# Query features and linear attention in tiled fp32 products in place of split products, with the order of the FFN phase written as words

## The chip, the cores and the metric

The kernel runs on one core of a Trainium2 chip. The metric is the device time of one execution in microseconds (us). The engines are named as the profile does: PE (TensorE, matrix products), DVE (VectorE), ACT (ScalarE), POOL (GpSimd), SP (SyncE, which issues all DMA transfers).

## The reference

Eight sequences ("pairs" below, since each is two tiles of 128 rows) of 256 tokens, width 512, 16 heads of 32. All in fp32:

```
xn = layernorm(x);  q = xn Wq' + bq;  k = ctx Wk' + bk;  v = ctx Wv' + bv      (16 heads of 32)
q' = relu(q_h Wqf');  k' = relu(k_h Wkf') * mask                                (64 features a head)
kv = k'^T v;  k_sum = sum k'                                                    (64 x 32, 64 a head)
x  = x + (q' kv / (q' k_sum + 1e-8)) Wo' + bo
x  = x + BitNet FFN of layernorm(x): 8 bit activations, ternary weights,
     up * relu(gate)^2, sub-layernorm, quantized again, down (512 -> 2048 -> 512)
```

## The kernel before

A planner (`Plan`, L79) takes every instruction as a step with its lane, its waits and a cost. PE's steps run in the order in which the code adds them. ACT, DVE, POOL and SP are ordered by list scheduling: a time by which PE needs each step is worked out backwards from PE's order with the table `COST`, and each engine takes what is ready and needed first. Semaphores are derived from the plan.

Products that need fp32 accuracy are written as three float32r products of high and low parts (`products`), so each operand has to be split on ACT (high) and DVE (low). A phase for the keys comes first (until about 125 us): for each pair, keys, values, key features (`features`, L546, already fp32 products in tiles of 32 rows by 64 columns, one for each of four row groups and two column groups) and the blocks k'^T v with k_sum in a 33rd column (`kv`, L566, tiles of 128 rows by 64 columns), kept in `kvc` for all pairs.

Then come eight pairs on the query side, with these blocks for pair a, named by their letters in the code after the change:

- X (`s1`, twice): transposes of the normalized rows, 4 each. W (`s2`): q, 48 products of 256 columns, then on ACT the bias and high part (`qoh`), on DVE the low part (`qol`), and from pair 2 on a further copy `qy` and four SBUF to SBUF DMA copies `qx`, `qy` that put high and low parts of two heads side by side.
- Q (`s3`): query features, 24 products of 256 columns in pairs 0 and 1, 16 from pair 2 on. ACT writes relu as the high part, DVE the low part (`aph`, `apl`, at a = 0 `wkh`, `wkl`).
- K (`kv_blocks`): high and low parts of this pair's kv, two heads side by side with zeros between (`kvh`, `kvl`).
- A (`s4`, once for each row tile): attention, for each of 8 head pairs 3 products of 66 columns, so 48 in all; DVE adds 1e-8, takes reciprocals and multiplies (`dn`, `rd`, `on`).
- T (`s5`): 4 transposes of the attention rows, high and low parts. S (`s6`): output projection, 12 products of 512 columns, then on DVE, POOL and ACT the residual, layernorm and quantization, and the DMA transpose `xqT`, on which the FFN of that row tile waits.
- L (`ln1`): layernorm of the next pair's rows into `xn`, the tile that A's rows also use.
- G i.h (`gate_up`): half h of the gate and up products of row tile i, 8 + 8 bf16 products of 512 columns. D i (`down`): 16 such products. The FFN runs one pair behind the attention.

`mix(main, side, lag, end)` spreads the side list over the main list. In the loop at L924 the 48 attention products of a pair, with the transposes T of its first row tile among them, are spread over G and D products, from 6 after the first on to 10 before the last. For pair 0 they are spread over values products. Pair 7 is ordered by the string `TAIL`. PSUM banks 0 to 3 belong to G, banks 4 to 7 are handed out in turn by `bank()`. Lines of the profile: L344 is the helper of nearly all products, L347 that of ACT, L350, L353 and L356 those of DVE, L612 the transposes, L581 `kv` and L558 `features`.

Of the kernel before, what the change touches and what calls it, by code (L numbers as in the profile page):

```python
# [10 lines left out]
F32 = mybir.dt.float32  # L11
# [25 lines left out]
TAIL = "D9 G12.0:a Q0123 K MG12.0:b,G12.1,D10 S0 S1 G13.0 G13.1 G14.0 G14.1 G15.0 G15.1 B012345 D11 D12 D13 D14 D15"  # L37
# [34 lines left out]
HOLDS = ("Y", "xbo", "kvh", "kvl")  # L72
HELD = ("kk", "kvl", "xn", "xm", "yb", "yk")
# [156 lines left out]
def xattn_bitffn_kernel(nc, x_d, ctx_d, wk_d, wv_d, wq_d, wo_d, feat_d, small_d, bv_d, bo_d, g_d, wg_d, wu_d, wd_d, out_d):  # L230
# [4 lines left out]
    with ExitStack() as es:  # L235
# [193 lines left out]
        dma("feat", 0.25, [], fraw, feat_d, "feat")  # L429
# [58 lines left out]

        def biased(tag, oqs, outs, k, bias, copy=None):

            for oq, src in zip(oqs, outs):
                act(f"{tag}.{oq}.hi", 0.4, [k, "small"], qoh[:, T * oq:T * oq + T], src, ACT.Identity, bias=bias[:, oq:oq + 1])
                if copy is not None:
                    act(f"{tag}.{oq}.copy", 0.4, [k, "small"], copy[:, T * oq:T * oq + T], src, ACT.Identity, bias=bias[:, oq:oq + 1])
            los = []
            copies = [f"{tag}.{oq}.copy" for oq in oqs] if copy is not None else []
            for oq, src in zip(oqs, outs):
                qs = slice(T * oq, T * oq + T)
                los.append(stt(f"{tag}.{oq}.lo", 0.4, [f"{tag}.{oqs[-1]}.hi", f"{tag}.{oq}.hi", k, "small"] + copies, qol[:, qs], src, bias[:, oq:oq + 1], f32(qoh[:, qs]), ALU.add, ALU.subtract))
            return los  # L500
# [45 lines left out]
        def features(b):  # L546


            for t in range(2):
                i = 2 * b + t  # L550
                for q in range(4):
                    for r in range(4):
                        for c in range(2):
                            waits = [f"kT{b}.{q}.all", "feat.raw"] + (bank_user[r] if t == q == c == 0 else [])
# [4 lines left out]
            for r in range(4):  # L559
# [3 lines left out]
                ready = [f"kf{2 * b + 1}.3.{r}.0", f"kf{2 * b + 1}.3.{r}.1", "small", "feat.raw", "feat.hi", "fpad.lo"]  # L563
                bank_user[r] = [stt(f"kf{b}.{r}.rows", 0.65, ready, dst, src, 0.0, on, ALU.max, ALU.mult)]

        def kv(b):  # L566
# [3 lines left out]
            for half in range(2):  # L570
                for pr in range(4 * half, 4 * half + 4):
                    for t in range(2):
                        for hd in range(2):
                            def call(half=half, pr=pr, t=t, hd=hd):
                                i = 2 * b + t
                                waits = [f"kf{b}.{r}.rows" for r in range(4)] + [f"v{b}.{t}.rows"] + (bank_user[base + half] if pr % 4 == t == hd == 0 else [])
                                rows = slice(64 * hd, 64 * hd + 64)
                                out = ps[rows, base + half, 33 * (pr % 4):33 * (pr % 4) + 33]
                                o = 256 * (2 * (pr % 2) + hd) + 64 * (pr // 2)
                                left, right = kp[:, t, o:o + 64], vt[:, i % 4, pr, 33 * hd:33 * hd + 33]  # L580
                                k = add("pe", f"kv{b}.{pr}.{t}.{hd}", 0.06, waits, lambda e: e.matmul(out, left, right, start=t == 0, stop=t == 1, tile_position=(0, 64 * hd)))  # L581
                                if pr % 4 == 3 and t == hd == 1:
                                    src = ps[:, base + half, 0:132].rearrange("p (c d) -> p c d", c=4)
                                    bank_user[base + half] = [act(f"kv{b}.{half}", 0.3, [f"kv{b}.{pr}.{t}.0", k], kvc[:, b, 4 * half:4 * half + 4, :], src, ACT.Copy)]
# [441 lines left out]
```

How the kernel before makes its waits and increments, by code:

```python
        def run(lane, eng):  # L199
            seen = {}
            for i in order.get(lane, []):
                _, name, _, waits, fn, dma = self.steps[i]
                need = {}
                for w in waits:
                    s, v = at[w]
                    if need.get(s, (0, None))[0] < v:
                        need[s] = (v, w)
                for s, (v, _) in need.items():
                    if seen.get(s, 0) < v:
                        eng.wait_ge(s, v)
                        seen[s] = v
                last = fn(eng)
                if dma is not None:
                    last.then_inc(dma_sems[dma], 16)
                elif name in at:
                    last.then_inc(sems[lane], 1)
# [6 lines left out]
        def sync(e):  # L223
            run("sp", e)
            e.wait_ge(dma_sems["out"], issued["out"])
```

## Time and profile before

| | |
|---|---|
| median of 3 runs | 454.1 us (453.23 to 454.24) |
| profiled execution | 454.95 us, span 453.2 us |
| PE busy | 439.6 us (97%), 4147 records |
| weight loads (PEld) | 342.4 us (76%) |
| DVE busy | 367.0 us (81%) |
| ACT busy | 298.0 us (66%) |
| POOL busy | 130.7 us (29%) |
| DMA | 45.61 MB, mean 101 GB/s |
| granted TensorE clock | 1.00 throughout |

The span runs from the first to the last instruction. Products are pipelined, so a record's busy time is longer than the distance between two starts; the distance is the cost. The last 44 us have no attention left.

### The profile page before, as it was taken

Reading aid. Unit: us, or ns where it says so; the run is one execution under the profiler, and the core shown is the slowest. Engines: PE = TensorE matmul, PEld = TensorE weight load, DVE = VectorE, ACT = ScalarE, POOL = GpSimd, SP = SyncE. Lnnn points to the kernel's source line nnn. Section 1 sums busy time; section 2 is a strip of 40 time slices with the busy share of each in tenths; the row PEclk is TensorE's granted clock in tenths of the full one; section 3 lists DMA queues with packets and bytes.
Section 4 is the critical chain, followed back from the end, with each engine's and each line's share of the span. In section 5 each row is a group of like instructions: output and inputs, shape, how many; then the busy total and the mean of one; then the engine's idle time right before and its main releaser. Section 6 shows DMA issues by size and latency. Waiting matters only on the chain.

```text
span 453.2 us, 10053 instructions
## 1 busy us (share of the span) xinstructions
PE 439.6 (97%) x4147; PEld 342.4 (76%) x4147; DVE 367.0 (81%) x635; ACT 298.0 (66%) x426; POOL 130.7 (29%) x280
## 2 busy tenths in 40 slices
PE   8999899999999999999999999999999999899995
PEld 5888889888999878958767776796877777684443
DVE  4735929358966989999989999898999898898992
ACT  5766969764232276786686768578575975738982
POOL 0000000005420644342342541444235054224430
PEclk9999999999999999999999999999999999999999
DMA  7991917423400210251223225025122123233045
GB/s 237 417 381 48 346 77 244 175 88 106 184 3 24 94 25 0 48 128 37 48 71 69 54 44 115 23 48 128 37 46 57 39 46 58 72 82 58 14 106 149
DMA packets 53085, 45.61 MB, mean 101 GB/s; under 512 B 43440, under 2 KB 44336, under 8 KB 51120
## 3 DMA queue, kind: packets, MB, share of 16 engines
q1 hardware_dynamic: 53040, 44.98, 34.1%
q8 instruction: 32, 0.52, 0.5%
q14 instruction: 13, 0.11, 0.1%
HBM read 27.14 MB, written 4.19 MB: 69 GB/s over the span
## 4 chain that ended last, share of the span: by engine, by line
PE 71%; DVE 13%; ACT 8%; issue 3%; DMA 2%; POOL 1%; SPq 0%; DVEq 0%; ACTq 0%
PE ps L344 63%; ACT rb L347 4%; PE ps L581 3%; DVE zb L350 3%; PE ps L558 3%; DVE tk L788 2%; PE ps L612 2%; ACT rbe L347 2%; ACT zb L347 1%; DMA xs<-in_wk_dram 1%; DVE qol L350 1%; DVE yqb L815 1%; ACT aph L347 1%; DMA yqTq<-yqb 1%; DMA xqT<-xqb 1%
## 5 line engine op out<-in xcount | busy, mean ns | idle before, releaser
L344 PE MATMUL ps<-tg,xqT 128*128 128x512 bf16 x256 | 68.1, 386 | 1.0 <-DMA xqT<-xqb 1.0
L344 PE MATMUL ps<-tu,xqT 128*128 128x512 bf16 x256 | 68.2, 385 | 0.0
L344 PE MATMUL ps<-td,yqT 128*128 128x512 bf16 x208 | 50.7, 385 | 0.0
L347 ACT ACTIVATE rb<-zb 128x1024 f32<-128x1024 f32 x29 | 30.6, 1055 | 28.8 <-DVE zb L350 28.8
L353 POOL TENSOR_SCALAR tk<-tk 128x1 f32<-128x1 f32 x96 | 37.4, 390 | 41.2 <-DVE tk L739 21.3
L347 ACT ACTIVATE zb<-zb,cm,tk 128x1024 f32<-128x1024 f32 x29 | 34.8, 1235 | 14.8 <-POOL tk L350 14.8
L347 ACT ACTIVATE rb<-ps 128x1024 f32<-128x1024 f32 x29 | 29.6, 1020 | 19.0 <-PE ps L344 18.1
L344 PEld LDWEIGHTS ps<-tu,xqT 128*128 128x128 bf16 x256 | 25.1, 98 | 21.5
L344 PE MATMUL ps<-kvh,apl 128*128 128x66 f32 x112 | 41.1, 367 | 0.0
L344 PE MATMUL ps<-kvh,aph 128*128 128x66 f32 x112 | 40.3, 359 | 0.3 <-DVE apl L356 0.3
L344 PE MATMUL ps<-kvl,aph 128*128 128x66 f32 x112 | 40.4, 361 | 0.0
L344 PEld LDWEIGHTS ps<-tg,xqT 128*128 128x128 bf16 x256 | 24.1, 99 | 21.0 <-issue 1.9
L350 DVE TENSOR_TENSOR zb<-zb,g_b 128x1024 f32<-128x1024 f32 x30 | 37.0, 1232 | 2.9 <-ACT rb L347 2.4
L350 DVE TENSOR_TENSOR zb<-ps,rb 128x1024 f32<-128x1024 f32 x29 | 35.2, 1213 | 4.5 <-PE ps L344 3.4
L350 POOL TENSOR_TENSOR tk<-tk 128x1 f32<-128x1 f32 x32 | 15.4, 480 | 78.7 <-ACT rb L347 65.3
L344 PE MATMUL ps<-aph,wkh 128*128 128x256 f32 x128 | 36.1, 286 | 0.9 <-ACT wkh L347 0.9
L788 DVE TENSOR_REDUCE tk<-zb 128x1 f32<-128x1024 f32 x30 | 36.4, 1212 | 0.3
L344 PE MATMUL ps<-aph,wqh 128*128 128x256 f32 x128 | 36.0, 282 | 0.3 <-DVE apl L350 0.3
L344 PE MATMUL ps<-apl,wkh 128*128 128x256 f32 x128 | 35.2, 279 | 0.7 <-issue 0.7
L350 POOL TENSOR_TENSOR xs<-xs,bo_b 128x512 f32<-128x512 f32 x16 | 24.5, 1540 | 39.0 <-DMA bo_b<-in_bo_dram 19.6
L344 PE MATMUL ps<-aph,wql 128*128 128x256 f32 x128 | 35.7, 279 | 0.0
L344 PE MATMUL ps<-apl,wqh 128*128 128x256 f32 x128 | 35.7, 279 | 0.0
(149 smaller groups left out, 1262.3 us busy)
## 6 DMA issues: line engine op xcount, KB each, us to landing
xs<-in_wg_dram SPq DMA_DIRECT2D x4, 1024.0 KB, 13.3
xs<-in_wu_dram SPq DMA_DIRECT2D x4, 1024.0 KB, 6.7
xs<-in_wd_dram SPq DMA_DIRECT2D x4, 1024.0 KB, 8.0
xs<-in_x_dram SPq DMA_DIRECT2D x8, 512.0 KB, 5.6
out_dram<-xs SPq DMA_DIRECT2D x15, 256.0 KB, 2.2
craw<-in_ctx_dram SPq DMA_DIRECT2D x7, 512.0 KB, 7.2
qoh<-qol SPq DMA_DIRECT2D x12, 128.0 KB, 2.2
qy<-qol SPq DMA_DIRECT2D x12, 128.0 KB, 2.4
```

The costliest lines, as they stand in the source:

```text
L344: return add("pe", name, cost, waits, lambda e: e.matmul(out, lhsT, rhs, start=start, stop=stop))
L347: return add("act", name, cost, waits, lambda e: e.activation(out, in_, func, **kw))
L350: return add(lane, name, cost, waits, lambda e: e.tensor_tensor(out, a, b, op))
L353: return add(lane, name, cost, waits, lambda e: e.tensor_scalar(out, a, s1, s2, op0, op1))
L558: add("pe", f"kf{i}.{q}.{r}.{c}", 0.015, waits, lambda e, out=out, left=left, right=right, at=(32 * r, 64 * c): e.matmul(out, left, right, ...
L581: k = add("pe", f"kv{b}.{pr}.{t}.{hd}", 0.06, waits, lambda e: e.matmul(out, left, right, start=t == 0, stop=t == 1, tile_position=(0, 64 ...
L612: add("pe", f"{tag}.{kc}", 0.11, (waits + bank_user[b] + ["small"]) if kc == 0 else [], lambda e, out=out, src=src: e.transpose(out, src, ...
L788: add("dve", f"ym{u}", 1.15, [f"Y{u}"], lambda e: e.tensor_reduce(col(M0 + h, i), zs, AX_X, ALU.max, apply_absolute_value=True))
L815: add("dve", f"yb{v}", 0.6, [f"yk{v}"] + war, lambda e, dst=dst, z=z: e.tensor_scalar(dst, z, MAGIC, None, ALU.subtract))
```

## The change

Query features and attention become plain fp32 products in tiles, as the key features were, and the split operands go with them.

- W writes q once, on ACT, with the bias, as fp32 `qT` (at a = 0 into `kT`). The low parts, the copy `qy` and the DMA copies are gone.
- Q is 16 products in 32x64 tiles with 256 moving columns: for each half of the quads, four row groups (heads) by two column groups. It needs four banks. ACT writes relu once, four steps of 512 columns, into `qf`.
- A is 64 products for a pair in 64x64 tiles with 33 moving columns straight from `kvc`: 8 head pairs, 2 heads (row groups), 2 column groups of 64 tokens, for each row tile. Each head parity has a bank of its own. K is gone with its memsets.
- `kvc` holds heads h and h + 4 together (`head`), so that rows 0 to 63 and 64 to 127 fit `qf`.
- A writes its rows to a tile of its own, `rows_of` (at a = 0 still `xn`), so L waits for the transposes X of the pair before.
- The order of pairs 1 to 7 is the list `FLOW`. Attention is no longer spread over FFN products: it stands in one piece between two halves.
- The feature weights are loaded directly into `fkr`, without the casts.

```diff
-TAIL = "D9 G12.0:a Q0123 K MG12.0:b,G12.1,D10 S0 S1 G13.0 G13.1 G14.0 G14.1 G15.0 G15.1 B012345 D11 D12 D13 D14 D15"
+FLOW = (
+    "G0.0:a Q G0.0:b A0 A1 G0.1 T0 T1 G1.0 G1.1 L S0 X0 X1 S1 W0 W1 D0",
+    "G2.0:a Q G2.0:b A0 A1 G2.1 T0 T1 D1 G3.0 G3.1 L S0 X0 X1 S1 W0 W1 D2",
...
+    "G10.0:a Q G10.0:b A0 A1 G10.1 T0 T1 G11.0 G11.1 L S0 X0 X1 S1 W0 W1",
+    "D9 G12.0:a Q G12.0:b A0 A1 G12.1 T0 T1 D10 S0 S1 G13.0 G13.1 G14.0 G14.1 G15.0 G15.1 B012345 D11 D12 D13 D14 D15",
+)
...
-HOLDS = ("Y", "xbo", "kvh", "kvl")
-HELD = ("kk", "kvl", "xn", "xm", "yb", "yk")
+HOLDS = ("Y", "xbo")
+HELD = ("kk", "xn", "xm", "yb", "yk")
...
-        dma("feat", 0.25, [], fraw, feat_d, "feat")
+        dma("feat", 0.2, [], fkr[:, :], feat_d[:, 0:384], "feat")
...
-                war = [f"oT{i - 2}.3"] if a else [f"warm{WARM - 1}"]
+                war = [f"oT{i - 2}.3" if a == 1 else f"xT{i - 2}.3"] if a else [f"warm{WARM - 1}"]
...
-                bank_user[b] = biased(f"qT{a}", (2 * o2, 2 * o2 + 1), [ps[:, b, 0:256], ps[:, b, 256:512]], k, bq, qy if a > 1 else None)
-                if a > 1:
-                    qs = slice(512 * o2, 512 * o2 + 512)
-                    dma(f"qx{a}.{o2}", 0.125, bank_user[b], f32(qoh[64:128, qs]), f32(qol[0:64, qs]), f"qx{o2}")
-                    dma(f"qy{a}.{o2}", 0.125, bank_user[b], f32(qy[0:64, qs]), f32(qol[64:128, qs]), f"qy{o2}")
+                bank_user[b] = [act(f"qT{a}.{oq}.all", 0.4, [k, "small"], (qT if a else kT)[:, T * oq:T * oq + T], ps[:, b, 256 * (oq % 2):256 * (oq % 2) + 256], ACT.Identity, bias=bq[:, oq:oq + 1]) for oq in (2 * o2, 2 * o2 + 1)]
+        def s3(a):
+            banks = [bank() for r in range(4)]
+            for q2 in range(2):
+                for r in range(4):
+                    for c in range(2):
+                        q = 2 * q2 + c
+                        rows, weights = slice(32 * r, 32 * r + 32), 256 + 64 * (r % 2)
+                        out = ps[64 * c:64 * c + 64, banks[r], 256 * q2:256 * q2 + 256]
+                        left, right = fkr[rows, weights:weights + 64], (qT if a else kT)[rows, T * q:T * q + T]
+                        waits = [f"qT{a}.{q}.all", "feat"] + (bank_user[banks[r]] if q2 == c == 0 else [])
+                        add("pe", f"qf{a}.{q2}.{r}.{c}", 0.0535, waits, lambda e, out=out, left=left, right=right, at=(32 * r, 64 * c): e.matmul(out, left, right, start=True, stop=True, tile_position=at))
+            war = [f"at{2 * a - 1}.7.1.{c}" for c in range(2)] if a else ctx_lo[NB - 1]
+            for r in range(4):
+                dst = qf[:, :].rearrange("p (q r t) -> p r q t", q=2, r=4)[:, r]
+                src = ps[:, banks[r], :].rearrange("p (q t) -> p q t", q=2)
+                bank_user[banks[r]] = [act(f"qf{a}.{r}.rows", 0.5, [f"qf{a}.1.{r}.0", f"qf{a}.1.{r}.1"] + war, dst, src, ACT.Relu)]
+        def s4(a, t):
+            i = 2 * a + t
+            banks = [bank(), bank()]
+            for pr in range(NP):
+                for hd in range(2):
+                    for c in range(2):
+                        rows, o = slice(64 * hd, 64 * hd + 64), T * pr + P * t + 64 * c
+                        waits = [f"qf{a}.{pr}.rows"] if pr < 4 and hd == c == 0 else []
+                        if pr == c == 0:
+                            waits = waits + bank_user[banks[hd]] + [f"kv{a}.0", f"kv{a}.1"]
+                        out = ps[64 * c:64 * c + 64, banks[hd], 33 * pr:33 * pr + 33]
+                        left, right = qf[rows, o:o + 64], kvc[rows, a, pr, :]
+                        add("pe", f"at{i}.{pr}.{hd}.{c}", 0.027, waits, lambda e, out=out, left=left, right=right, at=(64 * hd, 64 * c): e.matmul(out, left, right, start=True, stop=True, tile_position=at))
...
         features(last)
         listed += [6, 7]
         s2(0)
-        mix(main[4:8], [])
+        mix(main[4:12], [])
         listed += [0, 1, 2, 3]
         s3(0)
+        mix(main[12:18], [])
         listed += [0, 1, 2, 3]
-        mix(main[8:], s4(0, 0, 0.1) + s4(0, 1, 0.1), 4)
-        left = kv(last)
-        mix(left[:16], [])
+        s4(0, 0)
+        s4(0, 1)
+        mix(main[18:], [])
...
-        mix(left[16:], [])
+        mix(kv(last), [])
...
-            mix(main, side, 6, 10)
-            s5(a, 1)
...
+        for a, words in enumerate(FLOW, 1):
+            for word in words.split():
+                c, r = word[0], word[1:]
+                if c == "Q":
+                    s3(a)
+                elif c == "A":
+                    s4(a, int(r))
...
+                elif c == "W":
+                    s2(a + 1, (int(r),))
```

## Rows read from the trace of the kernel before

**Rows 1.** Windows: us, busy us (instructions) of each engine, granted clock, DMA

```profile
180.00:220.00 40.00, 40.00 (x262) 30.02 (x260) 37.73 (x67) 28.49 (x42) 15.52 (x32) 1.00 0.27 60
```

**Rows 2.** The page's chain that ended last, by engine

```profile
PE 71%; DVE 13%; ACT 8%; issue 3%; DMA 2%; POOL 1%; SPq 0%; DVEq 0%; ACTq 0%
```

**Rows 3.** Timeline of PE, pair 2: start, busy us, line, operation, count [idle before]

```profile
193.03 3.63 PE L344 MATMUL ps<-td,yqT 128*128 128x512 bf16 x16
...
199.76 0.47 PE L344 MATMUL ps<-qoh,fth 128*128 128x256 f32 x1
...
201.83 1.68 PE L344 MATMUL ps<-tg,xqT 128*128 128x512 bf16 x7
203.33 0.30 PE L344 MATMUL ps<-kvh,aph 128*128 128x66 f32 x1
...
212.75 0.60 PE L612 MATMUL ps<-small,xn 128*128 128x128 f32 x4
...
216.32 0.61 PE L344 MATMUL ps<-tg,xqT 128*128 128x512 bf16 x2
```

**Rows 4.** Timeline of PE, fp32 products in tiles, keys' side

```profile
107.13 2.06 PE L581 MATMUL ps<-vt,kp 128*64 128x33 f32 x64
109.12 0.50 PE L344 MATMUL ps<-woh,aph 128*128 128x512 f32 x1
...
112.07 1.60 PE L558 MATMUL ps<-fkr,kT 32*64 32x64 f32 x128
```

**Rows 5.** Timeline of PE, pair 0

```profile
132.12 0.28 PE L344 MATMUL ps<-qoh,fpd 128*128 128x256 f32 x1
...
134.95 0.40 PE L344 MATMUL ps<-woh,apl 128*128 128x512 f32 x1
...
136.11 0.19 PE L344 MATMUL ps<-kvh,wkh 128*128 128x66 f32 x1
...
144.03 0.31 PE L581 MATMUL ps<-vt,kp 128*64 128x33 f32 x4
...
148.16 0.50 PE L344 MATMUL ps<-woh,qoh 128*128 128x512 f32 x1 [0.55 <-DVE qol L350]
```

**Rows 6.** Timeline of PE, pair 1

```profile
167.92 0.38 PE L344 MATMUL ps<-kvh,aph 128*128 128x66 f32 x1
...
178.59 0.61 PE L344 MATMUL ps<-tg,xqT 128*128 128x512 bf16 x2
```

**Rows 7.** Timeline of PE, pair 7

```profile
386.04 1.89 PE L344 MATMUL ps<-tg,xqT 128*128 128x512 bf16 x8 [0.98 <-DMA xqT<-xqb]
388.49 0.35 PE L344 MATMUL ps<-qoh,fth 128*128 128x256 f32 x1 [0.57 <-issue]
...
391.79 0.38 PE L344 MATMUL ps<-kvh,aph 128*128 128x66 f32 x1
...
401.19 2.34 PE L344 MATMUL ps<-td,yqT 128*128 128x512 bf16 x10
```

**Rows 8.** Timeline of ACT

```profile
151.66 1.09 ACT L347 ACTIVATE aph<-ps 128x512 fp32r<-128x512 f32 x2 [3.48 <-PE ps L612]
...
163.64 1.02 ACT L347 ACTIVATE rb<-ps 128x1024 f32<-128x1024 f32 x1 [0.22 <-PE ps L344]
```

**Rows 9.** Timeline of DVE, the low parts of Wo

```profile
145.15 2.35 DVE L350 TENSOR_TENSOR wol<-xs,woh 128x1024 fp32r<-128x1024 f32 x2
```

**Rows 10.** Timeline of SP's queue

```profile
159.06 6.25 SPq L746 DMA_TRANSPOSE xqT<-xqb  x2
```

**Rows 11.** Groups by line, DVE: busy us, mean ns | idle before

```profile
L356 DVE SCALAR_TENSOR_TENSOR apl<-ps,aph 128x512 fp32r<-128x512 f32 x28 | 18.0, 683 | 0.9 <-ACT aph L347 0.9
```

**Rows 12.** Timeline of ACT, start of the last stretch

```profile
409.74 2.37 ACT L347 ACTIVATE zb<-zb,cm,tk 128x1024 f32<-128x1024 f32 x2 [5.13 <-POOL tk L350]
```

**Rows 13.** Timeline of PE, the last products

```profile
430.01 7.07 PE L344 MATMUL ps<-td,yqT 128*128 128x512 bf16 x32
...
446.72 3.67 PE L344 MATMUL ps<-td,yqTq 128*128 128x256 bf16 x32 [1.74 <-DMA yqTq<-yqb]
```

More of the change, by code:

```diff
@@ L487, in xattn_bitffn_kernel @@
         CW = wst[:, 12:13]
[L489 to L500, printed above, removed]
         def keys(b):
@@ L553, in features @@
                         for c in range(2):
-                            waits = [f"kT{b}.{q}.all", "feat.raw"] + (bank_user[r] if t == q == c == 0 else [])
+                            waits = [f"kT{b}.{q}.all", "feat"] + (bank_user[r] if t == q == c == 0 else [])
                             o = T * q + P * t + 64 * c
@@ L572, in kv, with call @@
                     for t in range(2):
-                        for hd in range(2):
-                            def call(half=half, pr=pr, t=t, hd=hd):
+                        for c in range(2):
+                            def call(half=half, pr=pr, t=t, c=c):
                                 i = 2 * b + t
[L576 to L582, printed above, removed]
+                                waits = [f"kf{b}.{r}.rows" for r in range(4)] + [f"v{b}.{t}.rows"] + (bank_user[base + half] if pr % 4 == t == c == 0 else [])
+                                h = head(pr, c)
+                                o = 256 * (h % 4) + 64 * (h // 4)
+                                out = ps[64 * c:64 * c + 64, base + half, 33 * (pr % 4):33 * (pr % 4) + 33]
+                                left, right = kp[:, t, o:o + 64], vt[:, i % 4, h // 2, 34 * (h % 2):34 * (h % 2) + 33]
+                                k = add("pe", f"kv{b}.{pr}.{t}.{c}", 0.06, waits, lambda e: e.matmul(out, left, right, start=t == 0, stop=t == 1, tile_position=(0, 64 * c)))
+                                if pr % 4 == 3 and t == 1 and c == 1:
                                     src = ps[:, base + half, 0:132].rearrange("p (c d) -> p c d", c=4)
-                                    bank_user[base + half] = [act(f"kv{b}.{half}", 0.3, [f"kv{b}.{pr}.{t}.0", k], kvc[:, b, 4 * half:4 * half + 4, :], src, ACT.Copy)]
+                                    bank_user[base + half] = [act(f"kv{b}.{half}", 0.3, [f"kv{b}.{pr}.1.{z}" for z in range(2)], kvc[:, b, 4 * half:4 * half + 4, :], src, ACT.Copy)]
                             calls.append(call)
@@ L616, in s1 @@
             i = 2 * a + t
-            b, k = transposes(f"xT{i}", t, [f"xn{i}"])
+            b, k = transposes(f"xT{i}", xn[:, t, :], [f"xn{i}"])
             src = ps[:, b, :].rearrange("p (a c) -> p a c", a=KC)
@@ L921, in xattn_bitffn_kernel @@
         s2(1)
-        kv_blocks(1)
-        for p in range(NB - 2):
-            a, n = p + 1, p + 2
-            early = (0, 1) if p == 0 else ()
-            s3(a, early)
-            mix(gate_up(2 * p, 0), [])
-            s3(a, [q for q in range(4) if q not in early])
-            if p:
-                kv_blocks(a)
-            side = s4(a, 0) + s4(a, 1)
-            side.insert(36, lambda: s5(a, 0))
-            main = gate_up(2 * p, 1) + (down(2 * p - 1) if 0 < p < NB - 3 else []) + gate_up(2 * p + 1, 0) + gate_up(2 * p + 1, 1)
-            mix(main, side, 6, 10)
-            s5(a, 1)
-            ln1(n)
-            s6(a, 0)
-            s1(n, 0)
-            s1(n, 1)
-            s6(a, 1)
-            s2(n)
-            if n < NB - 1:
-                mix(down(2 * p), [])
-        a = NB - 1
         rest = {}
```

164 lines of the change are left out of this document (49 added, 115 removed), and 3 rows, old and new, of the table FLOW.

## The prediction

> **What bounds the kernel now.** I read the windows first: between 180 and 220 us TensorE is busy for all 40.00 us and VectorE for 37.73, at granted clock 1.00 [rows 1]. The page's chain puts 71% of the span on PE and 13% on DVE [rows 2]. So until about 409 us the order of products on PE is the clock of the kernel: a product taken away is time gained, unless a wait takes its place. I then went through PE's timeline pair by pair [rows 3, 5 to 7], and last to the end, where ACT and DVE alternate on the chain.
>
> **The change, part by part, on PE.** *Old attention.* In pair 2, 48 attention products lie between the first at 203.33 and the last FFN products at 216.32, 12.99 us [rows 3]. The code puts 47 bf16 products there (64 in the mix, less 7 ahead and 10 behind). One costs 0.216 us (16 took 3.63, the last of them 0.38 by itself: 3.25/15) [rows 3], so 10.15; four transposes cost 0.43 (busy 0.60, less the 0.17 by which 3.63 exceeds 16 x 0.216). That leaves 2.4 us, 0.050 a product: spread out one by one they are cheap. Pairs 3 to 5 have the same mix. In pair 1 there are only 31 bf16 products to spread them over: 178.59 - 167.92 = 10.67, less 6.70 and 0.43, leaves 3.5 [rows 6]; pair 6 has the same mix. In pair 7, 401.19 - 391.79 = 9.40, less 23 x 0.216 and 0.46, leaves 4.0 [rows 7]. In pair 0 the stretch from 136.11 to 144.03 holds 11 values products of 0.232 ((136.11 - 134.95)/5) and leaves 5.4 [rows 5]. Sum: 5.4 + 2 x 3.5 + 4 x 2.4 + 4.0 = 26.0 us.
>
> *Old query features.* 24 products took 134.95 - 132.12 = 2.83 in pair 0 [rows 5]; pair 1 has the same 24. In pair 2, 16 took 201.83 - 199.76 = 2.07 [rows 3], and six pairs are like it: 12.4. Sum 18.1. Old total 44.1 us.
>
> *New products.* No query-side tile is in this trace, but the keys' side has fp32 products in tiles. Each appears as two records (64 in a features batch of the code, x128 in the row). In 32x64 tiles with 64 moving columns, 128 records take 1.60 us, 12.5 ns each; in 128x64 tiles with 33 columns, 64 take 2.06, 32 ns each [rows 4]. Block A of the new code has 64 products, 128 records, a pair, with 33 columns and four tiles in place of two. Bounds: 128 x 12.5 ns = 1.6 us (all four as parallel as the eight are) and 128 x 32 ns = 4.1 us (no better than the 128x64 ones). I take half of the second, 2.0, since twice as many tiles can be under way and the columns are the same. Block Q has 16 products, 32 records, of 256 columns. A 256-column fp32 record should stream 0.21 us, an estimate from the four transposes above (128 columns, 0.43/4 each, one record). With eight tiles side by side that is 32 x 0.21/8 = 0.85; with only the four row groups side by side 1.7. The 32x64 row speaks for more than four: 64 columns would stream 53 ns, and a record came every 12.5, so 4.3 in flight even with loads of weights on both sides of so short a product. I take 1.0. Going into or out of tiles costs 0.1: the product after the tiles is busy 0.50, where another of its kind takes 0.40 [rows 4, 5]. Four such edges a pair: 0.4. New sum per pair 2.0 + 1.0 + 0.4 = 3.4, times 8 is 27.2. Gross gain 44.1 - 27.2 = 16.9 us.
>
> The kernel's row of 12.5 ns a record also answers a floor on starts. The Trainium skill (TensorE: Matmul & The Clock Gate, "Wait — 56ns, not 53.3ns?") says that matmul starts never come closer than about 25 ns, however few columns. By that rule block A would take 128 x 25 ns = 3.2 us, 1.2 more a pair and 9.6 in all, and the time would be 452; this trace has records twice as dense as that, so it disagrees for tiles.
>
> **What takes part of it back.** *The wait in front of block A.* The new order is gate half of G, Q, up half of G (8 products, 1.73 us), A. A needs four Relu results on ACT, which come one after another: two 512-column ones took 1.09, 0.55 each [rows 8]. ACT first has the gate's own Relu, 1.02 [rows 8], which becomes ready just as Q starts and fills Q's 1.0. Then 4 x 0.55 + 0.3 of signalling = 2.5 us behind Q's end, against 1.73 + 0.1 + 0.4 (A's first twelve products) = 2.2: 0.3 of wait if ACT is free, and 1.3 if one more 1 us operation is ahead. ACT is busy 28.49 of 40 us [rows 1]. I take 0.7 a pair, bounds 0 and 2.0; 8 pairs, 5.6. Queued behind A's first product on PE is everything, so each of these waits is paid in full. *Pair 0.* S0 waits for the low parts of Wo, which can start only when the last values product is done; the two took 2.35 on DVE, and S0 started at 148.16 after 0.55 idle [rows 5, 9]. This distance stays, while the attention products that filled some of it go: 0.6 lost (0 to 1.5). *Pair 1.* The first FFN product now follows W directly. Before, it had 1.42 us of query features ahead of it, and the first xqT transpose was issued only at 159.06 [rows 10], on a chain that began with S0's end. S0's end to W's end stays the same, so up to 1.4 becomes visible; 0.7 taken, as DVE has less to do. Together 6.9.
>
> *What gets easier.* DVE loses the low parts of q, of the features (28 x 0.683 = 18.0 us in that row alone [rows 11]) and of the kv blocks. With 37.73 of 40 busy, DVE's queue is what makes things late. In pair 7 PE waited 0.98 for xqT and 0.57 in front of the query features, the place of the qx and qy copies that are gone [rows 7]: 1.5 gained (0 to 1.6). In the end stretch ACT starts late (idle 5.13, then two yk until 412.1) [rows 12] and has to be through the last gates; the last products start at 446.72 where PE alone, from 430.01 with four down blocks of 3.46, would be there at 443.9 [rows 13]. So at most 2.9 can come back, at least 0 since the order of words after pair 7's S1 is the same; I take 0.5. DMA copies qx, qy (SP), the two memsets (POOL) and three start-up casts (ACT) are hidden in the first two cases by the PE stretch beside them; removing them counts 0. ln1 writes to a tile of its own now and no longer waits for the output transposes; it had been on no wait of PE, 0. New planner costs only reorder ACT, DVE, POOL and SP; ACT's order is in the 0.7.
>
> Sum: 16.9 - 6.9 + 1.5 + 0.5 = 12.0. The profiled execution took 454.95, span 453.2, which is 0.85 over the median 454.1 of the runs shown. 454.95 - 12.0 = 442.95; by the median, 442.1. I say 442.
>
> **Rivals.** *A, tiles don't run side by side (ends slower).* The place is block A: if its records come every 32 ns as in the 128x64 row, it takes 4.1 instead of 2.0, 16.8 over all pairs, and 459; with Q at 1.7 as well, 464. It decides from 3.4 + 12.0/8 = 4.9 us a pair for Q, A and edges. For it: the old products, spread among bf16, cost only 0.050. Against it: the 12.5 ns row. *B, the waits take most of it.* Without the mix, each link Q, ACT, A, DVE, output transposes T stands in the open. At 2.0 in front of A and 0.3 at T it is 1.6 x 8 = 12.8 worse: 455, about the time before; at half of that, 448. For it: ACT runs operations of 1 us that can't be interrupted. Against it: ACT and DVE lose work. *C, no wait at all.* Q's results are in time, Wo and xqT too: 6.9 back, and the end gives 2.9: 433. *D, column tiles of one row group take turns.* The code issues both column tiles of a row group in succession, and Q takes 1.7: 5.6 worse, 448. The Trainium skill (TensorE: Matmul & The Clock Gate, "Part 3: Packing small matmuls — row/col tiling") says that a load of weights overlaps a running product only when its row group differs, which would make such turns. The 12.5 ns row has 4.3 records in flight at 53 ns, just over the four of that rule, so the trace doesn't exclude it.
>
> **How the numbers follow.** Forecast (waits near 0.7, tiles side by side) 0.53, its own range 437 to 446. A 0.10, B 0.12, C 0.12, D 0.13. The range that leaves out no more than 2 in 10 runs from 434 (close to C) to 453 (most of B). Within 0.2% (0.9 us, about what can be told from no change) lies a strip of B: 0.04. Slower: A and the rest of B, 0.11. Faster: 0.85.
>
> **What would show it.** In the timeline of PE, block A of pairs 2 to 5 should be 128 records within 2.0 us (4.1 is rival A), block Q 32 records within 1.0 (1.7 is D). Idle time of PE in front of A, released by ACT, of 0.3 to 1.3 (none is C, 2 is B). S1's end of pair 2 to that of pair 3 should shrink by 0.4 us only; the gain is at pairs 0, 1, 6 and 7. DVE's busy time between 180 and 220 should fall from 37.7 to near 33. The wait for xqT in pair 7 should be gone. The prediction is wrong if block A costs over 3 us, or if PE loses over 2 us in each pair to waits.

## The result, and the profile after

The kernel after takes 450.1 us (median of 4 runs, 449.26 to 450.7), the kernel before 454.17 (4 runs, 453.23 to 454.42). The ratio is 0.991, interval 0.9892 to 0.9928: faster by 0.9%, 4.1 us, where 12.0 was forecast. The profiled execution took 450.66 with a span of 448.6; before it was 454.95 and 453.2. So the span fell by 4.6.

First the windows (busy us of PE, PEld, DVE, ACT, POOL, then granted clock, DMA share, GB/s), which answer to [rows 1]:

```profile
180.00:220.00 40.00, 39.15 (x350) 25.31 (x354) 33.75 (x57) 25.17 (x35) 13.33 (x32) 1.00 0.31 61
...
380.00:420.00 40.00, 36.84 (x305) 19.80 (x308) 29.90 (x51) 26.48 (x34) 10.20 (x30) 0.96 0.22 50
```

DVE fell to 33.75, as forecast. But PE, which was busy for all 40.00 us, now stands still for 0.85 of them, and in the later window for 3.16, at a granted clock of 0.96. The page's chain shows the same, beside [rows 2]:

```profile
PE 44%; DVE 21%; ACT 14%; POOL 9%; issue 9%; DMA 3%; SPq 0%; DVEq 0%; ACTq 0%
```

PE's share fell from 71% to 44%. The work was removed from PE, and the chain now runs more often over DVE, ACT and POOL. Next PE's timeline in pair 0, where neither new block waits:

```profile
132.11 1.12 PE L643 MATMUL ps<-kT,fkr 32*64 32x256 f32 x32
133.16 0.50 PE L350 MATMUL ps<-woh,aph 128*128 128x512 f32 x1
...
134.75 2.35 PE L663 MATMUL ps<-kvc,qf 64*64 64x33 f32 x128
137.03 0.50 PE L350 MATMUL ps<-woh,aph 128*128 128x512 f32 x1
```

From start to start, block Q's 32 records take 1.05 us (1.0 forecast) and block A's 128 take 2.28 (2.0). With four edges of 0.1, Q and A cost 3.7 us in pair 0. Later on they are cheaper: in pair 2 (rows below) the stretch from G2.0's first product at 191.22 to the transposes T at 202.35 is 11.13 us. Less 32 FFN products of 0.216 and less the 0.97 that Q waits, 3.25 are left for Q, A and edges, against 3.4 forecast; A with its edges is 2.1 of it, 16 to 17 ns a record. The prices were nearly right; the loss lies between the blocks.

To place it, I cut the span at fixed points of PE's order: the first keys' product, the first S0 product of pair 0 (148.16 and 142.88), the eight transposes X (L605, before L612) of pairs 1 to 6, G13.0 (409.28 and 400.98), the end. X of pair 1 and of pair 6, before:

```profile
183.96 1.03 PE L612 MATMUL ps<-small,xn 128*128 128x128 f32 x8
...
371.92 1.04 PE L612 MATMUL ps<-small,xn 128*128 128x128 f32 x8
```

After:

```profile
178.49 1.03 PE L605 MATMUL ps<-small,xn 128*128 128x128 f32 x8
...
366.84 1.03 PE L605 MATMUL ps<-small,xn 128*128 128x128 f32 x8
```

| stretch (us) | before | after | change | forecast |
|---|---|---|---|---|
| to the first keys' product | 107.13 | 106.35 | -0.8 | 0 |
| to S0 of pair 0 | 41.03 | 36.53 | -4.5 | -3.5 |
| pair 1 (to its X) | 35.80 | 35.61 | -0.2 | -1.5 |
| pairs 2 to 5 (X to X) | 151.82 | 152.59 | +0.8 | -1.5 |
| pair 6 | 36.14 | 35.76 | -0.4 | -1.5 |
| pair 7 (to G13.0) | 37.36 | 34.14 | -3.2 | -3.5 |
| from G13.0 on | 43.92 | 47.62 | +3.7 | -0.5 |

The X of pair 5 stands at 335.78 and 331.08. The first line is no effect of the change: the start-up moves by up to 2.5 us between kernels that differ only later (S0 of pair 0 stands at 141.72 in experiment 2 and at 144.19 in experiment 6). Three places hold the miss: the end stretch (4.2), pairs 2 to 5 (2.3), pairs 1 and 6 (2.4).

**Pairs 2 to 5.** Pair 2 on all engines:

```profile
190.01 1.63 DVE L359 TENSOR_SCALAR xq<-xs,mv,rstd 128x512 f32<-128x512 f32 x1 [0.72 <-POOL rstd L356]
190.09 2.69 POOL L356 TENSOR_TENSOR xs<-xs,bo_b 128x512 f32<-128x512 f32 x2
...
191.22 1.89 PE L350 MATMUL ps<-tg,xqT 128*128 128x512 bf16 x8
...
191.56 1.76 DVE L774 TENSOR_SCALAR yqb<-zb 128x1024 bf16<-128x1024 f32 x1
...
193.04 0.67 PE L643 MATMUL ps<-qT,fkr 32*64 32x256 f32 x12
...
193.25 0.74 DVE L362 SCALAR_TENSOR_TENSOR xs<-ps,tk,xs 128x512 f32<-128x512 f32 x1
...
194.04 1.08 PE L643 MATMUL ps<-qT,fkr 32*64 32x256 f32 x20 [0.33 <-DVE xs L362]
...
202.35 1.04 PE L605 MATMUL ps<-small,rows_of 128*128 128x128 f32 x8
...
210.13 1.89 PE L350 MATMUL ps<-tg,xqT 128*128 128x512 bf16 x8
212.10 1.90 PE L350 MATMUL ps<-tu,xqT 128*128 128x512 bf16 x8
```

Q is broken after 12 of its records. Q needs four banks of PSUM; the fourth is the one in which the down block D stands, and it is free only when DVE has read D's result (the copy `y`, L362, to 193.99). From 193.04 to the end of Q at 195.12 are 2.08 us instead of 1.12: 0.97 lost (1.13 in pair 5). DVE comes late to `y` since two operations ahead of it take 1.63 and 1.76 us, while POOL adds `bo` to x (xbo, 2.69). The Trainium skill (SBUF — State Buffer, "SBUF: two separate sides") says that VectorE, when it works in a mode with two ports or reads two operands from SBUF, and GpSimd exclude each other from one shared pair of ports, and that the first holds it for its whole instruction. The rows look like that (1.63 and 1.76 us beside POOL's 2.69), and the third experiment below moves POOL's work away.

A second loss is smaller and no row gives it as idle time: the gate half of the second row tile starts at 210.13 and its up half at 212.10, 1.97 us for 8 products that take 1.73. That is 0.24 in each of pairs 2 to 5.

**Pairs 1 and 6.** In pair 1 PE waits in front of G0.0, within A and in front of an up half; in pair 6 block A is cut three times:

```profile
156.17 1.67 PE L350 MATMUL ps<-tg,xqT 128*128 128x512 bf16 x7 [0.97 <-DMA xqT<-xqb]
...
161.99 1.72 PE L663 MATMUL ps<-kvc,qf 64*64 64x33 f32 x104 [0.17 <-ACT qf L353]
...
173.99 1.90 PE L350 MATMUL ps<-tu,xqT 128*128 128x512 bf16 x7 [0.67 <-DVE sy L365]
```

```profile
348.90 0.31 PE L663 MATMUL ps<-kvc,qf 64*64 64x33 f32 x4 [0.31 <-ACT qf L353]
...
350.36 1.72 PE L663 MATMUL ps<-kvc,qf 64*64 64x33 f32 x104 [0.17 <-ACT qf L353]
...
362.35 1.90 PE L350 MATMUL ps<-tu,xqT 128*128 128x512 bf16 x7 [0.66 <-DVE zb L356]
```

A's wait in front and within makes its stretch 3.1, 3.6 and 3.5 us long in pairs 1, 6 and 7, so 1.0, 1.5 and 1.4 more than 2.1. The waits of 0.67 and 0.66 in front of G1.1's and G11.1's up halves (0.82 each from start to start) are new too, and were not in the forecast. The up half needs the banks that DVE empties of the half before; no experiment took this wait away, so why DVE is late there stays open.

**End stretch.** PE, then SP's queue:

```profile
410.12 3.30 PE L350 MATMUL ps<-tg,xqT 128*128 128x512 bf16 x8 [2.07 <-DMA xqT<-xqb]
...
415.26 1.89 PE L350 MATMUL ps<-tg,xqT 128*128 128x512 bf16 x7
```

```profile
405.08 1.83 SPq L781 DMA_TRANSPOSE yqT<-yqb  x1
406.96 6.84 SPq L705 DMA_TRANSPOSE xqT<-xqb  x2
```

G14.0 waits 2.07 us for the transpose xqT14, which stands behind yqT12 in SP's queue. Before, the order was the other:

```profile
413.35 1.20 SPq L746 DMA_TRANSPOSE xqT<-xqb  x1
414.65 1.72 SPq L822 DMA_TRANSPOSE yqT<-yqb  x1
```

Behind the wait the granted clock falls to half (the 1.2 GHz level):

```profile
411.00:412.00 1.00, 1.00 (x4) 0.36 (x3) 0.97 (x1) 0.70 (x1) 0.74 (x3) 0.50 0.00 0
...
413.00:414.00 1.00, 1.00 (x4) 0.34 (x3) 0.97 (x2) 0.54 (x1) 0.00 (x0) 0.58 0.17 35
```

G14.0's 16 products take 415.26 - 410.12 = 5.14 us; 16 products of G13.0 and G13.1 take 3.5 (402.71 to 406.17 is 3.46). So 2.07 of wait and 1.7 of clock make the 3.7 of the table. The two are not one cause, though. In experiment 3 the same wait stands, and the clock behind it stays at 1.00:

```profile
409.43 1.89 PE L350 MATMUL ps<-tg,xqT 128*128 128x512 bf16 x8 [2.07 <-DMA xqT<-xqb]
...
410.00:411.00 1.00, 1.00 (x7) 0.45 (x5) 0.97 (x2) 1.00 (x3) 0.45 (x2) 1.00 0.00 0
```

Experiments 2 (wait 2.07) and 6 (2.02) show no fall there either. The wait comes with the queue's order; the fall stood behind it in this execution and stands elsewhere in others.

### The profile page after: what moved, and what is told of

It is laid out like the page before. It is cut to its first block, busy times and chain, and to the rows that moved or that the text cites. A ratio compares the mean times of both kernels' runs of the same rounds, so it can differ in the third digit from the quotient of the medians.

```text
span 448.6 us, 11346 instructions
## 1 busy us (share of the span) xinstructions
PE 426.8 (95%) x4869; PEld 301.8 (67%) x4899; DVE 332.1 (74%) x554; ACT 282.5 (63%) x383; POOL 119.6 (27%) x278
## 4 chain that ended last, share of the span: by engine, by line
PE 44%; DVE 21%; ACT 14%; POOL 9%; issue 9%; DMA 3%; SPq 0%; DVEq 0%; ACTq 0%
PE ps L350 32%; DVE zb L356 5%; ACT rb L353 5%; POOL tk L359 4%; ACT zb L353 4%; DVE tk L747 4%; PE ps L574 4%; PE ps L663 3%; PE ps L547 3%; POOL tk L356 3%; DVE yqb L774 2%; DVE qol L356 2%; ACT qf L353 2%; DVE xs L362 2%; DMA xqT<-xqb 1%
## 5 line engine op out<-in xcount | busy, mean ns | idle before, releaser
L350 PE MATMUL ps<-tg,xqT 128*128 128x512 bf16 x246 | 59.9, 386 | 4.3 <-DMA xqT<-xqb 3.0
L350 PE MATMUL ps<-tu,xqT 128*128 128x512 bf16 x244 | 59.3, 381 | 2.9 <-issue 1.0
L359 POOL TENSOR_SCALAR tk<-tk 128x1 f32<-128x1 f32 x96 | 42.2, 441 | 40.7 <-DVE tk L698 24.7
L350 PEld LDWEIGHTS ps<-tu,xqT 128*128 128x128 bf16 x256 | 24.1, 98 | 34.9 <-DVE zb L356 4.6
L350 PE MATMUL ps<-td,yqT 128*128 128x512 bf16 x201 | 45.5, 379 | 0.5
L350 PE MATMUL ps<-aph,wkl 128*128 128x256 f32 x128 | 35.1, 278 | 0.0
L350 PEld LDWEIGHTS ps<-td,yqT 128*128 128x128 bf16 x208 | 19.8, 98 | 22.3
L359 POOL TENSOR_SCALAR lnv<-mv 128x1 f32<-128x1 f32 x32 | 9.4, 294 | 89.7 <-DVE mv L590 87.2
L356 POOL TENSOR_TENSOR tk<-tk 128x1 f32<-128x1 f32 x32 | 7.2, 224 | 96.3 <-ACT rb L353 82.7
L353 ACT ACTIVATE rb<-rb 128x1024 f32<-128x1024 f32 x29 | 30.8, 1061 | 0.7
```

The costliest lines, as they stand in the source:

```text
L350: return add("pe", name, cost, waits, lambda e: e.matmul(out, lhsT, rhs, start=start, stop=stop))
L353: return add("act", name, cost, waits, lambda e: e.activation(out, in_, func, **kw))
L356: return add(lane, name, cost, waits, lambda e: e.tensor_tensor(out, a, b, op))
L359: return add(lane, name, cost, waits, lambda e: e.tensor_scalar(out, a, s1, s2, op0, op1))
```

## The experiments

The first four ran on one chip (before: 454.49, 11 runs), the others on a second (before: 453.96, 9 runs). Each is an edit of the kernel after, but for the fifth.

### 1. The transpose of x14 first

```
-add("sp", f"yqT{i}", 1.8, [...] + war, ...
+add("sp", f"yqT{i}", 1.8, [...] + war + (["xq14.b"] if i == 12 else []), ...
-URGENT = {}
+URGENT = {"xqT14": 3.0}
```

> The changed kernel with one wait more: the transpose of yq of row tile 12 is issued only when xq14 is rounded (xq14.b), so that on SP's queue the transpose xqT14 goes first. Theory (the end stretch lost 3.7 us because xqT14 stood 0.9 us behind yqT12's 1.83 on SP and PE then waited 2.07 in front of G14.0 and fell to the lower clock): that wait shrinks to about 0.5, no low clock, G14.0 starts 1.6 earlier, the 16 products after it no longer take 3.1 us too long in all, and the time falls by 1.5 to 3: 447 to 448.6. Rival (the end stretch is set by ACT, which is busy with the yk and gate operations anyway, and PE's wait is only its echo): G14.0 starts earlier but the last product does not, time 449.5 to 450.5.

Measured: 449.08 (446.66 to 451.86), ratio 0.9888 (0.9853 to 0.9922), which overlaps that of the kernel after (0.9892 to 0.9928). PE and SP's queue:

```profile
409.85 1.89 PE L350 MATMUL ps<-tg,xqT 128*128 128x512 bf16 x8 [0.46 <-ACT rbe L353]
```

```profile
407.29 1.20 SPq L705 DMA_TRANSPOSE xqT<-xqb  x1
408.53 1.84 SPq L781 DMA_TRANSPOSE yqT<-yqb  x1
```

The wait fell from 2.07 to 0.46 and has another releaser, and from G13.0 on the kernel takes 44.3 us instead of 47.6. The order of SP's queue was the cause of the wait. The median hardly moved, and the low clock came elsewhere. The six runs fall into steps by their mean granted clock: 446.66 and 447.05 at 1.000, 448.6 and 449.56 at 0.996, 451.83 and 451.86 at 0.992. In the profile the fall stands behind block A of pair 6:

```profile
353.00:354.00 1.00, 1.00 (x4) 0.36 (x3) 1.00 (x3) 0.00 (x0) 0.00 (x0) 0.50 0.00 0
```

Pair 6 took 37.24 us instead of 35.76. One such fall goes with 1.5 us in the profile; a step of 0.004 in the mean clock goes with some 2.5 us of time.

### 2. The down block ahead of W

```
-"G2.0:a Q G2.0:b A0 A1 G2.1 T0 T1 D1 G3.0 G3.1 L S0 X0 X1 S1 W0 W1 D2"
+"G2.0:a Q G2.0:b A0 A1 G2.1 T0 T1 D1 G3.0 G3.1 L S0 X0 X1 S1 D2 W0 W1"   (D0 to D8 alike)
```

> The changed kernel with the words D0, D2, D4, D6, D8 moved in front of W0 W1 of their pair. Theory (block Q's fourth bank is the one that the down products have just used, and waits for their result y on DVE, 0.97 us in each of pairs 2 to 5): the wait goes, pairs 2 to 5 shrink from 38.1 to about 37.2 us each, time 446.5. In exchange qT of W1 (two ACT copies of 0.47) has only the gate half of G, 1.73 us, to be ready in; it should fit. Rival (PE waits there for DVE whatever the bank, as DVE's queue is late): Q's first product waits for qT or the wait shows up at another place, time 449 to 450.5.

Measured: 449.48 (five runs 448.04 to 450.94, one of 454.96 at a mean clock of 0.985), ratio 0.9891 (0.9873 to 0.991), not told apart from the kernel after by time. Pairs 3 to 5 take 37.18, 37.20 and 37.20 instead of 38.1: 0.93 each, the size of the wait. Q of pair 3 stands in one piece, and A follows without a wait:

```profile
230.99 1.12 PE L643 MATMUL ps<-qT,fkr 32*64 32x256 f32 x32
...
233.87 2.11 PE L663 MATMUL ps<-kvc,qf 64*64 64x33 f32 x128
```

So Q's fourth bank was what held pairs 2 to 5. But D0 now comes before yqT0 has landed (0.84), so that pair 2 takes 0.96 more, and pair 6 takes 0.78 more, where A waits 0.70 for ACT instead of 0.31. That gave back 1.7 of the 2.8 gained.

### 3. POOL's addition of bo later

```
-tt("pool", f"xbo{i}", 1.23, [f"xn{i}", "bo"], ...
+tt("pool", f"xbo{i}", 1.23, [f"xn{i}", "bo"] + ([f"at{2 * a + 1}.7.1.1"] if a > 1 else []), ...
```

> The changed kernel with POOL's additions xbo of pairs 2 to 7 made to wait for the last attention product of their pair; PE's order is the same. Theory (y is late because two DVE operations ahead of it, xq at 1.63 instead of 0.54 and yqb at 1.76 instead of 0.68, run beside POOL's xbo and are stretched by 1.1 us each): both are back at 0.54 and 0.68, y ends 1 to 2 us earlier, the 0.97 wait in Q is gone in pairs 2 to 5, time 446 to 447. Rival (the two are long for a reason of their own, or xbo stretches other DVE operations on the path at its new place): wait in Q unchanged or the same us lost elsewhere, time 449.5 to 451.

Measured: 447.53 (447.02 to 448.23), ratio 0.9848 (0.9835 to 0.9861). Groups of DVE (busy us, mean ns | idle before), after and here:

```profile
L774 DVE TENSOR_SCALAR yqb<-zb 128x1024 bf16<-128x1024 f32 x28 | 24.5, 878 | 3.6 <-ACT zb L353 3.4
L359 DVE TENSOR_SCALAR xq<-xs,mv,rstd 128x512 f32<-128x512 f32 x16 | 14.0, 876 | 5.7 <-POOL rstd L356 5.6
```

```profile
L774 DVE TENSOR_SCALAR yqb<-zb 128x1024 bf16<-128x1024 f32 x28 | 19.2, 688 | 4.4 <-ACT zb L353 4.3
L359 DVE TENSOR_SCALAR xq<-xs,mv,rstd 128x512 f32<-128x512 f32 x16 | 8.7, 544 | 7.7 <-POOL rstd L356 7.4
```

The same operations cost 10.6 us less on DVE with POOL away: the stretching is shown. It was not all of Q's wait, though. In pair 3, DVE's order now is both yqb, then y:

```profile
228.56 0.68 DVE L774 TENSOR_SCALAR yqb<-zb 128x1024 bf16<-128x1024 f32 x1
...
229.45 0.68 DVE L774 TENSOR_SCALAR yqb<-zb 128x1024 bf16<-128x1024 f32 x1
230.04 0.75 DVE L362 SCALAR_TENSOR_TENSOR xs<-ps,tk,xs 128x512 f32<-128x512 f32 x1
```

y ends at 230.79, and Q (230.11) takes 1.80 instead of 1.12. The pairs 2 to 5 gained only 0.07 to 0.3 each, pair 1 0.58, pair 6 0.49. With y directly behind two yqb, its place in DVE's queue is what is left, and the stretching was a part of the wait. By the ratios this edit alone gained clearly on the kernel after, 2.8 us.

### 4. Block A spread over the FFN products

The 128 records of a pair are issued in 16 groups of 8, each followed by FFN products, as the old attention was.

```
-"G2.0:a Q G2.0:b A0 A1 G2.1 T0 T1 D1 G3.0 G3.1 L ..."
+"G2.0:a Q MG2.0:b,G2.1,D1,G3.0,G3.1 L ..."   (M: one group of A after each two or three products)
```

> The changed kernel with the attention products of pairs 1 to 7 spread over FFN products as before the change, in 16 groups of four tiled products, transposes of the first row tile among them. Theory (each way into or out of tiles costs 0.1 us of PE, so in one piece is the right place for them): 30 more edges in each of 7 pairs, 3.0 us a pair less the 1 us of waits that spreading hides, time 464 (460 to 471). Rival (the new order with its open waits is what ate the gain, and tiles may be mixed with FFN products as cheaply as the old products were, 0.050 each): the waits of pairs 1 to 7 go and nothing is lost, time 440 to 445.

Measured: 471.8 (471.06 to 472.04), ratio 1.0381 (1.0367 to 1.0395), clock 1.000 in all four runs. Pair 2:

```profile
199.96 0.32 PE L666 MATMUL ps<-kvc,qf 64*64 64x33 f32 x8
200.21 0.39 PE L350 MATMUL ps<-tu,xqT 128*128 128x512 bf16 x1
```

21.7 us more than the kernel after, where 14 (10 to 21) was expected. The spreading adds 30 edges a pair in seven pairs, 210, so 0.10 us an edge, the value of the forecast. That is net of the waits that spreading hides. The rows give it directly too: from one group (200.96) to the next (201.97) are 1.01 us, less three FFN products (0.65) and 8 records of 16 ns (0.13), 0.23 for two edges. In this form one piece is right, which shows why the order had to change together with the products.

### 5. The new order with the old products

The kernel before, with its query features and attention (split products) each in one piece at the places of Q and A.

```
-s3(a, early)
-mix(gate_up(2 * p, 0), [])
+mix(g[:8], [])
+s3(a)
+mix(g[8:], [])
...
-mix(main, side, 6, 10)
+mix(s4(a, 0) + s4(a, 1), [])
+mix(gate_up(2 * p, 1), [])
```

> The kernel before, with its split products, but in the new order: in pairs 1 to 7 the 48 attention products stand in one piece between the two halves of the first row tile, with kv_blocks ahead of them and both output transposes behind the second half. Theory (the order by itself costs, and only the tiled products make up for it): in one piece an old attention product costs 0.11 to 0.12 us instead of 0.050 (pairs 2 to 5), 0.07 (1, 6) or 0.08 (7), which is 4 x 3.2 + 2 x 2.0 + 1.6 = 18 us more, and the waits for the low parts in front of the block come on top: 473 to 480. Rival (the order is neutral or helps, so the gain comes from it): 450 to 456.

Measured: 496.25 (491.59 to 498.44), ratio 1.0917 (1.0861 to 1.0972), with mean clocks of 0.962 to 0.976. The order by itself costs 42 us, more than the 19 to 26 expected. Part of it is clock: there are four stretches like this one, where the attention stands, some 13 us in all (4 x 7.00 x 0.46).

```profile
214.00:221.00 7.00, 6.75 (x28) 4.74 (x29) 4.95 (x13) 0.85 (x2) 0.00 (x0) 0.54 0.09 19
```

So the one-piece order is no gain of its own: it pays with tiled products (experiment 4) and costs with the old ones. How the other 29 us divide into dearer products and waits was not worked out.

### 6. Cover in front of A in pairs 1, 6 and 7

```
-"G10.0:a Q G10.0:b A0 A1 G10.1 T0 T1 G11.0 G11.1 ..."
+"G10.0:a Q G10.0:b G10.1:a A0 A1 G10.1:b G11.0:a T0 T1 G11.0:b G11.1 ..."
```

> The changed kernel with three words moved: in pairs 1, 6 and 7 the gate half of the next FFN half stands between block Q and block A, so that 16 products instead of 8 cover ACT's relu results; half of an FFN product group or of D10 is put in front of the transposes T. Theory (block A's stretch took 3.1, 3.4 and 3.5 us in these pairs against 2.1 in pairs 2 to 5, as it waited for the four relu steps on ACT, 1.0 + 1.3 + 1.4 = 3.7 us): the stretches are 2.1, 0.1 for one more pair of edges at most is paid, time 446 to 447. Rival (ACT's queue is only put off, the wait comes back at the next gate half or at T): 449 to 451.

Measured: 448.33 (448.27 to 450.51), ratio 0.989 (0.9868 to 0.9911), not told apart from the kernel after by time. In pair 1 A stands in one piece, and S0 of pair 0 to X of pair 1 took 34.53 instead of 35.61:

```profile
163.70 2.07 PE L663 MATMUL ps<-kvc,qf 64*64 64x33 f32 x128
```

Pair 2 gave back 0.85 of it at Q's bank, where the idle time between Q's two parts grew from 0.33 to 1.18. In pair 6 the wait only moved: the inserted gate half itself waits for ACT to empty a bank.

```profile
350.10 1.90 PE L350 MATMUL ps<-tg,xqT 128*128 128x512 bf16 x8 [0.51 <-ACT rb L353]
```

### 7. All four together

Experiments 1, 2, 3 and 6 in one kernel; D0 stands between W0 and W1.

> All four remedies in the changed kernel: xqT14 first on SP, POOL's xbo behind block A in pairs 2 to 7, down products in front of W (in pair 1 between W0 and W1), and the cover of block A in pairs 1, 6 and 7. If the causes are separate, their gains add up: 450.1 less 2.5 (queue), 2.6 (xbo), 2.8 (three pairs at 0.93) and 3.3 (cover) is 439. Rival (one shared queue, ACT's or DVE's, sets the pace of pairs 2 to 5 once PE's open waits are gone): the sum falls short, 443 to 446. In a run at granted clock 1.000 it should be 2 us below the median.

Measured: 442.33 (442.16 to 443.81), ratio 0.9752 (0.9733 to 0.9772), mean clock 0.999 to 1.000 in all five runs. It beats the kernel before by 11.6 us, and from the ratios the kernel after by 7. The waits at Q and in front of A are nearly gone, and the one in front of G14.0 fell from 2.07 to 0.63 and is for ACT:

```profile
229.82 1.12 PE L643 MATMUL ps<-qT,fkr 32*64 32x256 f32 x32
...
403.73 1.89 PE L350 MATMUL ps<-tg,xqT 128*128 128x512 bf16 x8 [0.63 <-ACT rbe L353]
```

Pairs 3 to 5 take 37.20 each, 0.8 less than before the change; pair 6 35.25. So the figure forecast for the change, 442, is reached, but only with four more edits. It lies between the theory (439) and its rival (443 to 446): the stretches that the single experiments were to remove add up to 3 us more than was gained. By their medians the parts were smaller: 1.0, 0.9, 2.8 and 0.9 us by the ratios, 5.6 in sum, less than the 7 together; in most runs of experiments 1 and 2 the clock fell somewhere. Two waits are left: pair 2 still takes 38.08 (Q waits 0.28 for ACT's qT), and the 0.71 in front of G11.1's up half remains.

### 8. Every attention product twice

```
+add("pe", f"ax{i}.{pr}.{hd}.{c}", 0.027, waits, lambda e, ...: e.matmul(out, left, right, start=True, stop=True, tile_position=at))
 add("pe", f"at{i}.{pr}.{hd}.{c}", 0.027, [], ...
```

> The changed kernel with every tiled attention product issued twice in succession to the same place (the work of block A is doubled, the result the same). Theory on the price (128 records in 2.1 us): 8 x 2.0 = 16 us more, 466. Theory on the clock (long stretches of nothing but tiled products are what the granted clock falls behind, since it fell after block A in the profiled executions of three variants and never in those of the kernel before or of the spread order): the mean clock is below 0.99 in most runs and the time above 468. Rival (only idle time of PE lowers the clock): clock 0.996 to 1.000 as before, time 465 to 467.

Measured: 476.1 (474.38 to 478.32), ratio 1.0489 (1.0457 to 1.0521): 26.0 us more than after where 16 was expected. The groups of PE and the end of one block:

```profile
L664 PE MATMUL ps<-kvc,qf 64*64 64x33 f32 x1024 | 33.2, 220 | 3.7 <-issue 3.7
L663 PE MATMUL ps<-kvc,qf 64*64 64x33 f32 x1024 | 33.2, 222 | 6.8 <-issue 6.5 <-ACT qf L353 0.2
```

```profile
207.52 0.34 PE L663 MATMUL ps<-kvc,qf 64*64 64x33 f32 x8 [1.46 <-issue]
```

"issue" is idle time in which the engine waits for nothing that the profile shows: 3.7 + 6.5 = 10.2 us, one gap of 1 to 2.5 us late in seven of the eight blocks of 256 records. The block of pair 3, without a gap, took 244.10 to 248.15, 16 ns a record. So 16 for the products and 10 for the gaps. The price of A is confirmed; no such gap is in the blocks of 128. The wait in front of G14.0 and the fall behind it (3.7 in the kernel after) aren't in this profile; two other falls, 1.7 us each, are, one behind the gap of 2.46 us in pair 6 and one behind a wait of 2.01 for the last transpose. The theory on the clock isn't decided: the mean clock was 0.989 twice and 0.993 twice, lower than the 0.996 to 1.000 of its rival, but the gaps are idle time too, so long tiled stretches and idle time were not separated.

## Why the prediction was wrong, point by point

- *Old products, 44.1 us; new ones, 27.2.* Right where it can be seen: 3.25 measured for the 3.4 a pair, 3.7 in pair 0. There 4.5 was gained against 3.5, as there is no wait in front of A (0.7) and the stretch from the last values product to S0 grew by 0.24 only (138.51 to 142.88 against 144.03 to 148.16) where 0.6 was taken. 0.1 an edge is confirmed by experiment 4.
- *Rivals A and D* (tiles don't run side by side; column tiles take turns) are refuted by A at 16 to 17 ns a record and Q at 1.05 us. The Trainium skill (TensorE: Matmul & The Clock Gate, "Wait — 56ns, not 53.3ns?") gives a floor of 25 ns between starts; for tiles the measurement is below it. *Rival C* (433) is out. *Rival B*, waits behind the links in the open, is in part what happened: 450.1 lies between its 448 and 455. But its places were not the ones. It had 16 us in front of A, where 3.9 were lost, and 0.3 a pair at T, where nothing was.
- *Wait in front of A, 0.7 x 8 = 5.6.* Measured 1.0 + 1.5 + 1.4 = 3.9 in pairs 1, 6 and 7, none in pair 0 and none in pairs 2 to 5. That Q's own wait gave ACT the time there isn't the reason: in experiment 2 Q doesn't wait, and A follows without a wait all the same. The term was too large in sum and stood at the wrong pairs.
- **A step that failed: "the order of words after pair 7's S1 is the same", so at least 0 in the end stretch.** PE's order was the same, SP's was not: the planner now put yqT12 ahead of xqT14. I had costed "new planner costs only reorder ACT, DVE, POOL and SP" at nothing. (Whether the new costs or the other steps of the plan turned the two round was not tried.) The order cost 2.07 of wait, of which 0.46 is there for ACT even with the order put right (experiment 1); with the 1.7 of clock behind it in this execution and the 0.5 hoped for, the stretch is 4.2 off the forecast.
- **The step that cost most: what Q waits for.** I asked what A needs (ACT's results) and not what Q needs: a fourth bank, free only after DVE's `y`. The price is 0.97 in each of pairs 2 to 4 and 1.13 in pair 5, 4.0 in sum (experiment 2). With the 0.24 in front of the up half, each pair grew by about 0.2 instead of shrinking by 0.4. Before, DVE did `y` at 197.48 in pair 2, ahead of both yqb, and the features began at 199.76, 3.3 us behind D's last product; now Q begins 1.8 us behind it, and `y` comes after a yqb.
- *The up halves of the second row tile* stood in no term: 0.82 in pairs 1 and 6 and 0.24 in each of pairs 2 to 5, 2.6 in sum.
- *Pair 1.* The wait for xqT0 was taken at 0.7 and is 0.97. With A's 1.0 and the 0.82 before the up half it eats 2.8 of the 3.1 (3.5 + 2.83 - 3.25) that the products give; 0.2 was gained, 0.1 is not assigned to a row.
- *Pair 7.* 3.5 forecast, 3.2 measured; the waits for xqT12 and for the copies are gone, A's is 1.4 instead of 0.7.
- *DVE near 33* was right (33.75), but its busy time held 10.6 us of stretching beside POOL, which a busy share doesn't tell apart from work.
- *The clock* was in no term, and in the profiled execution it is 1.7 us. It was 1.000 in all runs of the kernel before and of experiment 4, where small products are spread among large ones, and 0.995 to 0.999 in those of the kernel after.

So the forecast had the gross gain right (44.1 - 27.2) and the losses wrong. It took 6.9 for waits in front of A, at S0 and for xqT0, where about 5 were measured, and nothing for Q's bank (4.0), the up halves (2.6), SP's order (2.1) and the clock (1.7).

## What to carry to other kernels

When small products are gathered into one block, list for the block everything it needs, the banks it writes included, and read for each who frees it and what that engine has queued ahead. An order left "the same" must be checked on every queue that a planner can touch: one swapped pair of transposes cost 2 us, half as much as the whole change gained. Then undo the waits one at a time and all together, since some alone gave back a part at the next link (0.9 to 2.8 us alone, 7 together).

## What the runs showed of the hardware

- Records of fp32 products (two for each product) start every 16 to 17 ns in 64x64 tiles (33 columns) and every 12.5 ns in 32x64 tiles (64 columns) [rows 4]. In Q's eight tiles, with 256 columns, they take 33 ns each. By the prediction's estimate of 0.21 us for one such record alone, more than six are under way at once, so column tiles of one row group run side by side.
- Going from tiles to the full array and back costs 0.10 us an edge, over 210 edges (0.23 for a pair of edges in the rows of experiment 4).
- A DVE TENSOR_SCALAR out of SBUF took 1.63 us instead of 0.54, and 1.76 instead of 0.68, beside a TENSOR_TENSOR on POOL.
- PE's granted clock fell to the 1.2 GHz level for 3 to 4 us behind a stretch of small tiled products that had waits in it, or behind the 2.07 us wait, and for 7 us in experiment 5 where the split attention products stood in one piece. Neither place is enough by itself: behind the same wait of 2.02 to 2.07 the clock stayed at 1.00 in experiments 2, 3 and 6, and the same kernel ran at 1.000 and at 0.992. What makes it fall in a given run stays open.
- Late in seven of eight blocks of 256 tiled records PE stood idle for 1 to 2.5 us, for nothing that the profile shows. Why was not tried.
